# 16-bit target table, updates for a further pass on Pool, last group in four tiles: a graph attention layer

## What is computed

```
w_e   = silu(ef_e @ W1r + b1r) @ W2r + silu(ef2_e @ W1s + b1s) @ W2s + b2r + b2s
alpha = sum over the 16 dims of each of 8 heads (Q[dst] * w_e * K[src]) / 4 * cutoff_e
out   = segment_sum(alpha * V[src], dst) / 16
y     = layernorm(x + out)          (no gain, no bias)
```

## Time and profile before

| | us |
|---|---|
| median of 3 runs | 1994.96 (1991.69 to 1996.93) |
| the profiled execution | 1993.38, its span 1992.0 |
| PE busy | 1726.2 (87%) |
| DVE busy | 1626.7 (82%) |
| POOL busy | 1492.8 (75%) |
| ACT busy | 576.0 (29%) |
| mean DMA share in most slices | 0.5 |

### The profile page before, as it was taken

One profiled execution on the slowest core, in us unless ns is written; L12 is line 12 of the kernel. 1 busy time (PEld: TensorE's weight loads), 2 busy tenths in 40 slices (PEclk: granted clock), 3 DMA queues, 4 the chain that ended last, 5 costly groups with the idle time before them and its releaser, 6 DMA issues. The chain is left out here.

```text
span 1992.0 us, 56803 instructions
## 1 busy us (share of the span) xinstructions
PE 1726.2 (87%) x14497; PEld 1256.5 (63%) x14497; DVE 1626.7 (82%) x4334; ACT 576.0 (29%) x1019; POOL 1492.8 (75%) x1565
## 2 busy tenths in 40 slices
PE   8799999999898898888898888888888888888887
PEld 7566666666666566666666655666666656666665
DVE  5589988989888878888887878888888878888787
ACT  5332323222222222222222322222222222222222
POOL 6777777777777777777777777777777777777775
PEclk9799999999999989998999999999989989999888
DMA  9755555555555555555555555555555555555553
GB/s 327 253 158 159 161 159 152 156 160 160 155 152 162 160 156 151 161 156 150 161 144 161 147 159 155 149 158 147 159 145 159 155 149 149 156 157 149 158 146 94
DMA packets 197258, 319.01 MB, mean 160 GB/s; under 512 B 82965, under 2 KB 110342, under 8 KB 196934
## 3 DMA queue, kind: packets, MB, share of 16 engines
q0 software_dynamic: 74304, 202.47, 35.5%
q1 hardware_dynamic: 113564, 105.88, 18.4%
q10 hardware_dynamic: 9066, 7.03, 1.5%
HBM read 300.46 MB, written 14.74 MB: 158 GB/s over the span
## 5 line engine op out<-in xcount | busy, mean ns | idle before, releaser
L615 POOL DMA_INDIRECT kvt<-kvtab,srcS x1532 | 1466.5, 957 | 473.4 <-issue 465.8
L713 ACT ACTIVATE hs<-bank,B 128x512 f32<-128x512 f32 x806 | 510.5, 684 | 1370.8 <-issue 766.0
L653 PE MATMUL bank<-W2r,hs 128*128 128x128 f32 x3224 | 499.2, 302 | 10.6 <-ACT hs L713 10.3
L653 PEld LDWEIGHTS bank<-W2r,hs 128*128 128x128 f32 x3224 | 423.5, 205 | 89.4 <-issue 71.3
L877 DVE TENSOR_TENSOR t<-bank,kvt 128x512 f32<-128x512 f32 (+1 forms) x397 | 266.2, 671 | 251.5 <-DMA kvt<-kvtab,srcS 136.9
L653 PE MATMUL bank<-W2s,hs 128*128 128x128 f32 x3224 | 455.0, 287 | 0.0
L653 PEld LDWEIGHTS bank<-W2s,hs 128*128 128x128 f32 x3224 | 423.6, 205 | 0.0
L668 PE MATMUL bank<-msg,oh 128*32 128x128 f32 x3224 | 179.8, 294 | 225.2 <-DVE accT L808 222.4
L668 PEld LDWEIGHTS bank<-msg,oh 128*32 128x32 f32 x3224 | 72.1, 110 | 416.5 <-issue 379.6
L894 DVE TENSOR_REDUCE bank<-t 128x32 f32<-128x512 f32 x403 | 280.1, 695 | 13.9
L630 PE MATMUL bank<-eft,W 32*128 32x512 f32 x1612 | 275.9, 672 | 2.9 <-ACT kvh L448 2.4
(11 more groups left out here) (100 smaller groups left out, 674.7 us busy)
## 6 DMA issues: line engine op xcount, KB each, us to landing
kvA<-kvtab ACTq DMA_DIRECT2D x3968, 1.0 KB
eft<-in_ef SPq DMA_DIRECT2D x102, 512.0 KB, 7.3
kvS<-kvtab SPq DMA_DIRECT2D x3200, 1.0 KB
kvt<-kvtab,srcS POOLq DMA_INDIRECT x1532
dbt<-dst SPq DMA_DIRECT2D x102, 192.0 KB, 6.3
qwt<-qtab SPq DMA_DIRECT2D x403, 24.0 KB
kvtab<-kvt SPq DMA_DIRECT2D x24, 256.0 KB, 7.4
qtab<-qx SPq DMA_DIRECT2D x12, 384.0 KB, 6.0
```

Of the source, the lines that this page charges most:

```text
L615: pool.indirect_dma_start(kvt[:, (g - HX) % KS, t, :], None, kvtab, bass.IndirectOffsetOnAxis(ap=srcS[:, g * TG + t:g * TG + t + 1], axis= ...
L653: pe.matmul(WB[g % 2][:, t * D:(t + 1) * D], hs[:, g % HS, j, t * 128:(t + 1) * 128], w2[:, :], start=(j == 0 and t == 0), stop=False, ski ...
L713: act.activation(hs[:, g % HS, j, :], HB[i % 4][:, :], ACT.Silu, bias=B1[:, j:j + 1]).then_inc(m_si, 1)
```

## The change

1. The target table holds 16-bit integers instead of bytes: dst16, dbt and the compare's input are int16, twice the bytes in each broadcast and in the table's write. basep is the plain sum of base and partition index; nodep and the low bytes are gone. ACT's load of cutS no longer waits for the conversion, as dst is read to another place.
2. The updates for a further pass are made on POOL, behind the gathers, base and basep after all of ot, rel after all of oh, basei and baseq after the sum of group 400.
3. The last group (402) is left out of the loop over groups. Its gathers have a semaphore for each tile; the fourth reads and writes 42 rows, as there are 426 edges left. DVE works it tile by tile (`last_tile`), with collects and sums of the groups before between the tiles, and PE's scatter waits for each tile's message.

```diff
-    dst8 = nc.dram_tensor("dst8", [NG, G], u8, kind="Internal").ap()
+    dst16 = nc.dram_tensor("dst16", [NG, G], i16, kind="Internal").ap()
...
-        dbt = sb("dbt", [128, DS, 4, G], u8)
+        dbt = sb("dbt", [128, DS, 4, G], i16)
...
-            link(dve.tensor_scalar(nodep[:, :], base[0:WP, :], pidx, None, ALU.add))
-            dve.tensor_copy(basep[:, :], low_byte(nodep)).then_inc(s_win, 1)
+            dve.tensor_scalar(basep[:, :], base[0:WP, :], pidx, None, ALU.add).then_inc(s_win, 1)
...
-                    dve.tensor_copy(low_bytes, low_byte(dbi)).then_inc(s_db, 1)
+                    dve.tensor_copy(db16[:, :], dbi[:, :]).then_inc(s_db, 1)
...
+                if g == LG:
+                    for t in range(gathered(g)):
+                        n = rows_of_last(t)
+                        pool.indirect_dma_start(
+                            kvt[0:n, (g - HX) % KS, t, :], None, kvtab,
+                            bass.IndirectOffsetOnAxis(ap=srcS[0:n, g * TG + t:g * TG + t + 1], axis=0),
+                        ).then_inc(l_kv[t], 16)
+                    break
...
+                    if g == LG:
+                        n = rows_of_last(t)
+                        pe.wait_ge(l_msg, t + 1)
+                    m = pe.matmul(strips(g)[32 * t:32 * t + W, 0:D], oh[0:n, g % MS, t, :], msg[0:n, g % MS, t, :],
...
+            def last_tile(t):
...
+                dve.tensor_tensor(t1[0:n, s, t:t + 1, :], tiles(WB[s][:, :])[0:n, t:t + 1, :], kv[:, :, 0:D],
+                                  ALU.mult).then_inc(l_t1, 1)
+                dve.wait_ge(l_t1, t + 1)
...
-                if g == NE - 2:
-                    window(NE - 2)
-                    window(NE - 1)
-                    next_rel()
-                    next_base()
...
+            window(LG)
+            accumulate(NE - 4)
+            collect(NE - 3)
+            dve.wait_ge(m_w, NE)
+            dve.wait_ge(m_q, NE)
+            last_tile(0)
+            accumulate(NE - 3)
+            last_tile(1)
+            collect(NE - 2)
+            last_tile(2)
             accumulate(NE - 2)
-            collect(NE - 1)
...
+            last_tile(3)
+            collect(LG)
+            accumulate(LG)
             dve.wait_ge(m_acc, NE)
-            dve.wait_ge(m_up, 6)
-
+
+            last_start = 4 * ((NE - 1) // 4)
+            pool.wait_ge(m_ot, NE)
+            pool.tensor_scalar(base[:, :], base[:, :], float(W), None, ALU.add).then_inc(m_up, 1)
+            pool.tensor_scalar(basep[:, :], basep[:, :], float(W), None, ALU.add).then_inc(m_up, 1)
+            pool.wait_ge(m_oh, NE)
+            pool.tensor_scalar(rel[:, :], rel[:, :], -float(W), None, ALU.add).then_inc(m_up, 1)
+            pool.wait_ge(m_up, 1)
+            pool.wait_ge(m_q, last_start + 1)
+            pool.wait_ge(m_acc, last_start + 1)
+            pool.tensor_copy(basei[:, :], base[0:1, :]).then_inc(m_up, 1)
+            pool.tensor_scalar(baseq[:, :], base[0:1, :], float(QROW), None, ALU.mult).then_inc(m_up, 1)
+            pool.wait_ge(m_up, 5)
```

98 lines of the change are left out of this document (48 added, 50 removed).

## The result

The changed kernel took 1984.32 us in the median of five runs (1982.95 to 1987.42), against 1991.69 for the kernel before in five runs on the same chip (1988.90 to 1996.93): a ratio of 0.9961, 95% interval 0.9944 to 0.9978. It is faster by 7 us, a little more than the 0.3% that the prediction called telling. The prediction said 1992.9 in a range of 1988 to 2000. It was wrong, and too pessimistic by 8.6 us.

What follows compares the result with a forecast made beforehand. Pool's chain of gathers was taken to bound the kernel. Start +1.0, stalls -6.6 and end +3.5 gave -2.1 us: 1993.4 becomes 1991.3, with 1.6 for the median 1992.9; range 1988 to 2000.

Steps and rivals of the forecast that it cites:

- The start, +1.0: Before the loop: the larger target table and first broadcast delay the loop's start, and Pool at group 20, by 1.0 us.
- The stalls, -6.6: In the loop: gathers starting during the 512-column compare lose less once it is 16-bit, 8.8 us becoming 2.2.
- The bound, 0 to -8.8: Limits on the loop's stall gain: from nothing to all 8.8 us lost at the 512-column compare after 110 us.
- The end, +3.5: After the last gather: Pool's library load and updates make it the last engine, adding 3.5 us.
- rival A: At the end: library load short or overlapped, under 4.5 us, VectorE last at +0.7; sum -4.9, median 1990.1; chance 0.24.
- The library load: Between Pool's last gather and its first update: loading code for Pool's arithmetic, priced at 7.3 us.
- The offset, +1.6: Whole kernel: the median of the runs set 1.6 us above the profiled execution.
- The forecast: Whole kernel: the likeliest case, Pool last at the end, sum -2.1 us, own range 1990 to 1996; chance 0.42.
- 1.28 to 13.4: At the end: us of the only code or table load a row shows, and of the slowest transfer row.
- "faster": Whole kernel: the outcome of a time under 1989.0 us, distinguishable from no change; chance 0.18.

## Why the prediction was wrong

*The start, +1.0.* In the first pair of profiles -0.4. The later start of the loop is seen on ScalarE, as about +1.3 from two profiles against seven; that it reaches Pool in full at group 20 is not seen, where all profiles but the one at 113.62 lie within 1.2 us of each other, and the first pair stands the other way round. The step is half borne out and its size on Pool stays open.

*The stalls, -6.6.* This is the step that failed, as a size. The part that the prediction worked out was nearly right: compare 0.34 us as said (0.25 ns a column where the 8-bit one takes 0.51, so the doubling takes place), its stalls 9.0 to 3.0, -6.0 against -6.6. What it left out is as large. It took the stalls at the 4x32 compare (5.2 us, "another 65 start inside L767") as a constant; they fell by 3.3, to 1.9. The 1.5 us in L877 (22 gathers) went as well, and so did the one stall of 0.63 at the last gather, which came from L813. This one needs no update to leave VectorE: with the 16-bit table alone it is gone too (0.95 at 1963.28), as Pool is done before the update of rel begins at 1964.77. Together 6.0 + 3.3 + 1.5 + 0.6 = 11.4 of the 12.0 measured. The 1.5 us are the 512-column compare's own: these gathers begin in L877 but 0.37 to 0.46 us before that compare, which puts off their second moment, and the prediction counted only those that begin inside. So the compare's own part was -7.5. Nor do gathers last "until it ends", as the prediction says, but 0.82 us longer, and that leaves a third of the stalls inside the compare and not a quarter: the stretch in which a start is delayed, from 0.10 us on, shrinks from 0.25 to 0.12 us, but 46 gathers still fell into it where 65 did before. The bound, 0 to -8.8, was drawn around one line of a mechanism that works at three more places of the trace; it should have gone to the whole 16 to 17 us.

*The end, +3.5.* The size was near (+2.8) by luck; the mechanism was rival A's, VectorE last, and A's own price was +0.7. The library load was 0.1 us instead of 7.3. The Trainium skill's figure of about 6 us for a first call to a freshly loaded kernel (GPSIMD Engine Reference, "Instruction dispatch") is not seen in front of these instructions either; no run here shows for which calls it holds. Pool's operations took 8.6 us instead of 5.7, mostly since rel took 4.28 and not 2.7. And Pool waited 1.0 us for the last compare of the cut. Pool was done 9.6 us behind its last gather, not 14.0. VectorE's last sum started 12.4 us behind it, where the prediction's own reckoning for it gives 1985.9 - 0.2 - 1974.65 = 11.05. Of the 1.35 between, the tiles are 0.74: they took 6.74 instead of 6.0. Here the prediction's sum is wrong in itself: four tiles of 1.46 are 5.84, and the three small operations between them, 0.19, 0.29 and 0.19, would have made it 6.5.

*The offset, +1.6.* The median was set above the profiled execution because it was so for the kernel before in three runs (1994.96 against 1993.38). In five runs its median is 1991.69, below, and the profiled execution of the changed kernel is its own median. This is 1.6 of the 8.6 us; the start is 1.4, the stalls 5.4, the end 0.7, and the 0.5 us more outside the span go the other way. Between the medians, a change of -2.1 us was forecast and -7.4 measured.

*The chances.* Rival A held 0.24, with the reasoning that nothing else wants Pool then. The forecast preferred the load because no row showed it and transfers of hundreds of KB were the nearest rows. A bound from both sides was given, 1.28 to 13.4; the truth lay below both. Why the load costs so little is not shown; code that is there already would be a case for which the lower end is zero, and the bound did not allow for it. The time that came lies below the 1989.0 of "faster", which had 0.18, and below 1986.9, the least that A was given.

## What to carry to other kernels

- Where Pool only issues gathers and bounds the kernel, look for every VectorE instruction that a gather's start can meet, and count what all of them cost, also for gathers that begin before the instruction. Making one of them shorter also shifted where gathers meet the others, and here that was worth 3.3 us beside the 7.5 of the shortening itself.
- Splitting a step into tiles pays only where the engine would otherwise wait for data. If its rows have long landed, it is pure fixed cost: 3.5 us on VectorE for four tiles here, 2.6 of it in the tail, since an operation on a quarter of the columns takes 0.28 us and not a quarter of 0.69, and a tile with a third of the rows is not cheaper.
- Work moved to an idle engine can still slow the busy one. An update on Pool under which a VectorE compare with two SBUF inputs began made it 2.67 us instead of 0.28, so put a long one behind the last of them.

## What the runs showed of the hardware

- A 96-partition compare from 16-bit to 16-bit goes at 0.25 ns a column, from 8-bit, with the same 0.21 us fixed, at 0.51 (0.344, 0.405 and 0.477 us).
- Pool's tensor_scalar in f32 takes about 0.2 us and 2.5 ns a column: 4.28 us for 1616 columns, 1.23 to 1.26 for 404 in 128 partitions, 1.22 to 1.36 in 96, 0.24 for 12; one row of 404, to integers, is no cheaper, 1.22. VectorE does the 1616 in 1.00.
- VectorE's 128x128 tensor_tensor with both inputs in SBUF took 0.28 us alone, 0.42 to 0.48 when it began 0.2 to 0.3 us into a Pool update of 404 columns and 2.67 when it began 0.8 us into one of 1604.
- An indirect gather of 128 rows, 0.946 us, has a moment 0.13 us behind its start that three compares of VectorE put off to their own end: a tensor_scalar from 8 bits, one from 16 bits, and a tensor_tensor with two SBUF inputs. The longest delays were 0.26 us by a compare of 0.48, 0.18 by one of 0.41, and 0.13 by those of 0.34 and 0.28. A second moment at 0.83 us was put off by those of 0.48 and 0.41. Gathers that start with the compare, less than 0.1 us into a tensor_scalar or 0.03 into the tensor_tensor, are not delayed.
- Going from gathers to arithmetic cost Pool 0.1 us.
- The median gather was 0.946 or 0.949 us, a difference of 4 us over the loop. It need not be the chip's: on each of the three chips of 3.1 ms both values occur, from one kernel to the next. On those three the row copies of SP and ScalarE stood idle between instructions, and the same kernel took 3.1 ms.
